# Order of TensorE's work in layer 1's attention: a batch's scores ahead of the transposes of the batch two back

## What is computed

```
q_r    = (((norm(x) @ Wq.T) per head) @ w_kc_q) @ W_qr       # 16 heads, 64 wide
k_r    = rope(ctx) @ W_kr                                    # 375 keys, 64 wide
scores = q_r @ k_r.T                                         # 112 x 375 per batch and head
attn   = softmax(scores)                                     # over the 375 keys
ctx_c  = attn @ rope(ctx)                                    # 112 x 128
x      = x + tanh(g) * ((ctx_c @ w_kc_kv.T, heads joined) @ Wo.T)
```

## Time and profile before

| | us |
|---|---|
| median of 3 runs | 1037.68 (1036.01 to 1040.25) |
| the profiled execution | 1040.03 |
| its span, first to last instruction | 1038.0 |
| attention of layer 1, first scores to last weighted sum | 595.8 to 851.2 |
| pairs 1 to 6 of it | 625.97 to 817.10 |
| pair 7 and what is behind it | 817.10 to 851.2 |

### The profile page before, as it was taken

How to read it: one execution, slowest core, us unless ns; L and a number is a source line. 1 busy time by engine, 2 the same in 40 slices (tenths; PEclk the granted TensorE clock), 3 DMA queues, 4 the chain that set the end, 5 groups by cost and what they waited for, 6 DMA issues and landing times. The chain is left out here.

```text
span 1038.0 us, 19579 instructions
## 1 busy us (share of the span) xinstructions
PE 957.6 (92%) x6132; PEld 567.3 (55%) x6141; DVE 664.6 (64%) x1180; ACT 528.3 (51%) x1238; POOL 519.8 (50%) x652
## 2 busy tenths in 40 slices
PE   3679999999999999799989899999999979989998
PEld 1335555556565555444444567767777644444443
DVE  4788778787878777388677666676667643423012
ACT  2255666666666656400377267777677752116400
POOL 4477777676877777304224356666666641200000
PEclk9899999999999999999999899999999999999999
DMA  8213223131324211352020210222202014005001
GB/s 250 65 38 115 69 85 102 52 114 55 117 54 114 63 38 49 120 190 100 3 80 31 85 62 28 71 71 71 64 12 65 1 41 184 9 1 172 0 31 40
DMA packets 30344, 75.56 MB, mean 73 GB/s; under 512 B 4967, under 2 KB 11239, under 8 KB 28126
## 3 DMA queue, kind: packets, MB, share of 16 engines
q1 hardware_dynamic: 24706, 66.31, 20.4%
q10 hardware_dynamic: 5596, 8.70, 3.0%
HBM read 63.98 MB, written 3.68 MB: 65 GB/s over the span
## 5 line engine op out<-in xcount | busy, mean ns | idle before, releaser
L1222 POOL TENSOR_SCALAR scratch<-scratch,rinv 112x375 f32<-112x375 f32 x256 | 154.4, 616 | 139.3 <-DVE rinv L1062 139.3
L925 ACT ACTIVATE scratch<-ps,mxn 112x375 f32<-112x375 f32 x256 | 144.0, 570 | 36.5 <-DVE mxn L1057 35.0
L1057 DVE TENSOR_REDUCE mxn<-ps 112x2 f32<-112x750 f32 x128 | 119.6, 935 | 41.9 <-PE ps L718 41.4
L1203 POOL TENSOR_TENSOR scratch<-scratch 128x448 f32<-128x448 f32 x64 | 110.6, 1738 | 42.3 <-DVE scratch L1080 27.1
L772 PE MATMUL ps<-xnT,scratch 128*128 128x448 f16 x576 | 124.1, 363 | 6.5 <-DVE scratch L1136 3.6
L759 PE MATMUL ps<-scratch,kvn_hi 125*128 125x224 f16 x768 | 120.0, 261 | 5.3 <-DVE scratch L1102 2.3
L1214 POOL TENSOR_TENSOR scratch<-scratch 128x375 f16<-128x375 f32 x128 | 115.3, 901 | 10.9
L744 PEld LDWEIGHTS ps<-ident,scratch 112*125 112x125 f32 x768 | 100.9, 189 | 35.4 <-issue 26.7
L744 PE MATMUL ps<-ident,scratch 112*125 112x112 f32 x768 | 105.4, 273 | 9.3 <-DVE scratch L1125 9.2
L1125 DVE TENSOR_TENSOR scratch<-ps,scratch 125x672 f16<-125x672 f32 x128 | 108.7, 849 | 4.9 <-ACT scratch L935 4.9
L1080 DVE TENSOR_TENSOR scratch<-ps,ropeq 128x448 f32<-128x448 f32 x192 | 110.0, 615 | 2.1 <-PE ps L772 1.7
(11 more groups left out here) (168 smaller groups left out, 1479.1 us busy)
## 6 DMA issues: line engine op xcount, KB each, us to landing
scratch<-in_wq SPq DMA_DIRECT2D x16, 512.0 KB, 4.4
scratch<-in_wo SPq DMA_DIRECT2D x16, 512.0 KB, 3.6
wabs<-in_w ACTq DMA_DIRECT2D x32, 256.0 KB, 3.0
scratch<-in_w SPq DMA_DIRECT2D x8, 1024.0 KB, 4.9
scratch<-in_W SPq DMA_DIRECT2D x8, 1024.0 KB, 6.5
scratch<-scratch SPq DMA_DIRECT2D x64, 112.0 KB, 2.2
scratch<-in_kcq SPq DMA_DIRECT2D x8, 512.0 KB, 3.5
scratch<-in_qr SPq DMA_DIRECT2D x32, 128.0 KB, 3.0
```

What stands on the lines that cost most here:

```text
L925: last = nc.scalar.activation(prob[0:S, s % 2, hh, :], scores_ps[0:S, hh, 0:L], ACT.Exp, bias=mxn[0:S, s % 2, hh:hh + 1], accum_out=rsum[0 ...
L1057: nc.vector.tensor_reduce(mxn[0:S, s % 2, :], scores_ps[0:S, :, 0:L], AX_X, ALU.max, negate=True).then_inc(max_done, 1)
L1203: nc.gpsimd.tensor_tensor(roped[:, u % 2, rows], roped[:, u % 2, rows], turned[:, rows], ALU.add)\
L1222: last = nc.gpsimd.tensor_scalar(prob[0:S, s % 2, hh, :], prob[0:S, s % 2, hh, :], rinv[0:S, s % 2, hh:hh + 1], P_SCALE, ALU.mult, ALU.mult)
```

## The change

In each of the eight lists of TensorE for layer 1 the first two entries change places. The waits inside `scores` and `turn` are as before and move with them. The lists of the other three engines and all lists of layer 0 stay.

```diff
 ], [
-    [TURN, SCORES, ("S", 0), ("K", 2), ("Q", 1)],
-    [TURN, SCORES, ("S", 1), ("K", 3), ("G", 0), ("U", 0)],
-    [TURN, SCORES, ("S", 2), ("K", 4), ("W", 0)],
-    [TURN, SCORES, ("S", 3), ("K", 5), ("M", 0)],
-    [TURN, SCORES, ("S", 4), ("K", 6), ("F", 0)],
-    [TURN, SCORES, ("S", 5), ("K", 7), ("R", 0), ("Q", 0)],
-    [TURN, SCORES, ("S", 6), ("K", 0), ("U", 1)],
-    [TURN, SCORES, ("S", 7), ("K", 1), ("F", 1)],
+    [SCORES, TURN, ("S", 0), ("K", 2), ("Q", 1)],
+    [SCORES, TURN, ("S", 1), ("K", 3), ("G", 0), ("U", 0)],
+    [SCORES, TURN, ("S", 2), ("K", 4), ("W", 0)],
+    [SCORES, TURN, ("S", 3), ("K", 5), ("M", 0)],
+    [SCORES, TURN, ("S", 4), ("K", 6), ("F", 0)],
+    [SCORES, TURN, ("S", 5), ("K", 7), ("R", 0), ("Q", 0)],
+    [SCORES, TURN, ("S", 6), ("K", 0), ("U", 1)],
+    [SCORES, TURN, ("S", 7), ("K", 1), ("F", 1)],
 ])
```

## The result

| | median us | runs | ratio to before (95% interval) |
|---|---|---|---|
| after, first taking (before: 1037.55) | 1049.86 | 4 | 1.0135 [1.0111, 1.016] |
| after, second (before: 1037.31) | 1050.94 | 6 | 1.0129 [1.0108, 1.0149] |
| after, third (before: 1037.86) | 1051.60 | 5 | 1.0136 [1.0117, 1.0154] |

The differences of the medians are 12.3, 13.6 and 13.7 us; 16.6 were forecast, so the three medians lie 2.7 to 4.4 us under the forecast of 1054.3 and inside its range. The first profiled execution of after took 1049.72 us, with a span of 1047.7.

The account below looks back on a forecast made before the run. The loop was taken as bound by TensorE's list, 31.86 us a pair. Loop +10.9, pair 0 +1.5, pair 7 +4.3 and tail -0.1 sum to +16.6 on 1037.68, giving 1054.3 us; range 1045.5 to 1060.0.

Parts of the forecast that it names:

- the ring: Closed chain per slot: scores, transposes, weighted sum, its copy, exponentials, next scores; 4.14 us in the loop, 4.05 outside.
- slot 3, bound by TensorE: Slot with `M` in each loop pair: stays bound by TensorE's work, 4.46 plus 0.06, so 4.52 us.
- slot 6, bound by the bank of `Q`: Loop slot where the weighted sum could start at 715.15 but the bank frees at 715.30: 4.32 us.
- pair 7: Last pair, where TensorE has less to do: slots 0 to 6 go from 24.02 to 28.35 us, +4.3.
- (a): Transposes between scores and weighted sum: add 0.83 less 0.03 us, making scores to copy 2.55 in the loop.
- my low end: Lower bound: transposes' weight load hidden (0.74 us), scores' wait 0.06; loop slots 4.01, together +10.1 us.
- (b): Scores wait for the exponentials before overwriting their banks: 0.13 us from exponentials' end, bounds 0.06 to 0.14.
- (c): ScalarE and VectorE: the transposes' copy starts later but stays hidden ahead of the weighted sum's copy, 0.3 us to spare.
- What would show it: Expected signs: scores waiting for ScalarE, about 10 us in the loop, 0.6 a slot in pair 7; TensorE about 94% busy.
- faster rival: In pair 7, scores use the transposes' pause for VectorE: about 0.44 us saved per slot, 1034.6 in all; chance 2%.
- the covered wait: TensorE's work ahead of the scores hides their wait: loop unchanged, only pair 7 pays +4.3 us, 1042; chance 6%.
- the late copy of the transposes: ScalarE's copy of the transposes ends last and pushes the weighted sum's copy: 1059 at 0.1 past the slack; chance 7%.

## Why the prediction was right, and where it was off

| term | forecast | in the traces |
|---|---|---|
| slot of the ring in the loop | 4.14 | 4.09 to 4.12 |
| slot 3, bound by TensorE | 4.52 | 4.50 |
| slot 6, bound by the bank of `Q` | 4.32 | 4.32 |
| six loop pairs | +10.9 | +9.25 |
| pair 0 | +1.5 | +1.4 |
| slot of the ring in pair 7 | 4.05 | 4.00 |
| pair 7 | +4.3 | +4.1 |
| tail | -0.1 | -0.1, +0.6 or +1.3 by the clock |
| sum | +16.6 | +14.7; timed 12.3 to 13.7 |

- *The mechanism* held. Scores wait for the exponentials, the exponentials for the copy, the copy for TensorE. Taking the copy out of the ring gave back 12.3 us, and single slots paid by how late their exponentials were. The slots came out one by one within 0.06 us of the forecast, so the sum isn't right by luck.
- *The mis-sized term* is (a), the transposes between scores and weighted sum. I took 0.83 less 0.03. From the transposes' load (710.23) to the weighted sum's first matmul (710.98) it is 0.75, so scores to copy is 712.13 - 709.65 = 2.48, not 2.55; my low end had 2.49. The f32 load that starts together with its matmul behind the scores costs this distance next to nothing: the step takes 0.74 where that load was hidden (709.66 to 710.40 in before). The row of pair 7 from which I took 0.83 ends at a load of scores, which isn't hidden; here the weighted sum follows, and its load starts at 710.87, 0.11 ahead of its matmul. With 2.48 + 0.25 + 1.22 + 0.14 the ring is 4.09. The six ring slots of a pair are together 0.25 us shorter than forecast, 1.5 us over the loop and nearly all of the 1.65 that the loop was off by.
- *The rule on tiling* (the Trainium skill, TensorEngine Tiling (Array Packing), Key Properties: a change of mode drains TensorE). The number of changes is equal in both orders, and no run counts a drain by itself. I had concluded that only the load behind the scores is exposed. The rule doesn't say so, since the change into 64-row tiles is one as well, and the traces speak against it: the load of the scores itself starts with its matmul in both orders. The 0.06 a slot that I took from an exposed load behind the scores does appear on average in the two kernels with early exponentials, but for another reason, the 0.10 in front of the scores. That size was right by luck.
- *(b)*, the wait, was right: 0.14 from the end of the exponentials (713.60) to the matmul that follows the load at 713.71 (713.74), as in the earlier trace rows.
- *(c)* was right: the transposes' copy at 711.17 ends at 711.90, 0.23 ahead of the sum's.
- *What would show it*: the wait of the scores in the loop has 2.2 us on the list, not 10, and TensorE's share is 97%, not 94%. That expectation trusted a view that can't show short pauses. In pair 7 the named wait is 1.17, not 0.6; the pause that the transposes had there before, 0.44 in the earlier trace rows, has moved into it.
- The faster rival fell: pair 7 lost in every slot. So did the covered wait and the late copy of the transposes.

## What to carry to other kernels
An engine that is 99% busy is only the bound as long as no ring through the others is longer than its turn. Before moving a step ahead of another, add up the ring that the move closes, including what the *other* engines do in order: here ScalarE's list put the exponentials behind a copy whose input now came later, so earlier scores bought nothing and moved their wait into TensorE. If such a move is wanted, move the consumer's order with it; here that order alone, without the move, was the gain, 2.0 us in the traces.

## What the runs showed beyond that
- A wait of TensorE of 0.1 to 0.4 us behind matmuls may not be in the list of waits. The load of weights shows it: idle "issue" in front of a load, and a load that starts 0.1 us behind the end of what it needs.
- A slot's length isn't its engine's work: 3.99 us were 3.81 and such a wait, and stalls elsewhere absorbed it.
- The start of layer 1's attention moved between 590.3 and 596.9 us in the traces of one and the same kernel, though no edit touches the stages ahead of it. The mean granted clock up to there was 0.986, 0.977 and 0.980 in the three traces of after, with starts at 590.34, 596.39 and 596.92: the clock goes with most of the difference but doesn't order the last two. One per cent of this kernel is 10 us, so stretches with a full clock are needed to see the single terms.
